# A one-core attention and expert kernel: spreads moved to the head of each slot, norm rows joined, transpositions in 64-row halves

## Chip, core and metric

One Trainium2 chip, one of its cores. The time is microseconds on the device for one execution, from the first to the last instruction and what lies around them; the median of several executions counts.

## What is computed

Input x is (4, 64, 128, 128) in float32: 4 images, 64 channels, 16384 pixels each.

```python
x = x + _L0_conv_ref(_ln_c(x), ...)     # linear attention, 8 heads, over the pixels of an image
t = _to_tokens(x)
t = t + _L0_ffn_ref(_ln_t(t), ...)      # top 2 of 8 experts per pixel, each 64 x 64
```

`_ln_c` and `_ln_t` normalise each pixel over its 64 channels. Attention: keys and queries are relu(W x + b), context = keys x values summed over an image's pixels, attended = context x queries, then a 1x1 convolution. Experts: softmax over the router's logits, the best two renormalised, sum of gate times (token @ expert_w + expert_b).

## The kernel before

The pixels of an image are cut in two halves (S = 2, on partitions 0-63 and 64-127), these in pieces of 1024 pixels (NP), so there are 32 **groups** of 2 x 1024 pixels. A hand-written software pipeline runs over 49 **steps** n of four **slots** k each. In step n each part works on its own group: `L_COLS`, `L_TURN` and so on say how many steps after its loading a group comes to it; the experts come last (`L_EXPERTS` = 17). Steps 17 to 31 hold all parts, the first 17 only the front, the last 17 chiefly routing and experts. A slot holds two **iterations** of the experts; an iteration is one pair of experts (of 4) for one u (512 of the 1024 pixels) of both halves.

Parts, with the lines of the profile:
- rows: square x on GpSimd (L422), TensorE sums it to rows of statistics (L986, copied by ScalarE L497), transposes them to columns (L1006, copied L504); VectorE makes the deviations (`x_deviations`, L654-657, and after ScalarE's root L642-644).
- `turn_x` (L911) transposes x, eight 128x128 blocks; VectorE multiplies by the deviation (`normalise`, L676) into xnT; `turn_back` (L921) transposes this back, ScalarE copies it to xn (L492).
- `make_keys` (L936, L943), `sum_up` (L974, keys times xnT; `add_sums` L688), `make_queries` (L960), `attend` (L1020), `residual` on VectorE (L720), its square on ScalarE (L532); `fold`, once per image, makes the attention matrix.
- routing: the same rows and columns for logits (L986, L515, L1006, L523); `gates`, 27 small VectorE operations for two groups at once, spread over slots by `gates_by_phase`, with ScalarE's root, exponent (L543) and two copies; `turn_gates` (L1045) makes rows of gates again, copied to `grows` (L565).
- experts: `broadcast` (L1059) spreads the gates of a pair over the partitions (the **spread**); for half s=0 VectorE multiplies (`product`, L816), for s=1 ScalarE copies (L571) and GpSimd multiplies (L431); `experts` multiplies the **products** by the weights (L1073, L1076) onto a bias (L1070); after four iterations `result` (L826) adds x1 and stores.

Each engine works in program order. PSUM has six rotating banks for all of this: `bank_uses` lists the uses in order, use i takes bank i mod 6, and TensorE may fill it when use i-6 has been read. The bias matmul waits for `result` of the former u. Rings of four tiles (`R_Z`) hold the products.

Within a slot each engine first did the slot's part, then the spread or product of the next slot's iterations, then TensorE the experts:

```python
                    for i in iterations(n, k + 1):
                        broadcast(i)
                    for i in iterations(n, k):
                        experts(i)
```

## Time and profile before

| | |
|---|---|
| median of 3 executions | 705.34 us (703.17 to 705.60) |
| profiled execution | 708.03 us, span 706.2 us |
| TensorE busy | 647.4 us (92%), mean granted clock 0.99 |
| VectorE | 532.2 us (75%) |
| ScalarE | 428.5 us (61%) |
| GpSimd | 396.5 us (56%) |
| DMA engines | about half busy |

The busy share of TensorE is that of matmuls that lie over one another, so it does not say how close the engine is to its peak; start-to-start distances are used below. "Idle" in a row is the time in which the row's engine stood still just before it, and the arrow names what ended that.

### The profile page before, as it was taken

What the parts mean: (1) busy time and instruction counts of PE and PEld (TensorE: products, weight loads), DVE (VectorE), ACT (ScalarE), POOL (GpSimd) and SP (SyncE); (2) the same over time, 40 slices, a digit from 0 to 9 for tenths busy, and PEclk for the clock granted to TensorE, in tenths of its full rate; (3) what the DMA queues carried; (4) which work ended last, traced back from release to release, by engine and by line L of the source; (5) the groups of instructions that cost most, each with busy time, mean ns of one, the idle gap of its engine ahead of it and who ended that gap; (6) DMA issues with size and microseconds to landing.
All of it is one profiled execution on the core that took longest, in us unless ns stands there. A gap on an engine that the chain in (4) does not pass through costs nothing.

```text
span 706.2 us, 20616 instructions
## 1 busy us (share of the span) xinstructions
PE 647.4 (92%) x7846; PEld 302.0 (43%) x7846; DVE 532.2 (75%) x1176; ACT 428.5 (61%) x852; POOL 396.5 (56%) x350
## 2 busy tenths in 40 slices
PE   3898999799999999999999999999989889896786
PEld 1676766444544444444544444444322223231221
DVE  3443456878788988888788988867889998978853
ACT  2354556857566676657576776756656666564542
POOL 7132342165456566565456566555657667575785
PEclk9999999999999999999999999999999999999999
DMA  6232544655565555555566564444656555454442
GB/s 141 61 75 71 130 122 122 169 145 123 136 151 135 136 140 125 127 136 123 133 150 148 123 148 99 98 111 107 149 130 152 120 120 135 102 131 97 107 104 46
DMA packets 32660, 86.16 MB, mean 122 GB/s; under 512 B 7650, under 2 KB 7826, under 8 KB 32562
## 3 DMA queue, kind: packets, MB, share of 16 engines
q1 hardware_dynamic: 32082, 84.64, 50.7%
q8 instruction: 63, 1.03, 0.7%
q0 software_dynamic: 288, 0.19, 0.1%
q14 instruction: 35, 0.29, 0.1%
q10 hardware_dynamic: 192, 0.01, 0.0%
HBM read 34.47 MB, written 16.78 MB: 73 GB/s over the span
## 4 chain that ended last, share of the span: by engine, by line
PE 68%; DVE 13%; ACT 10%; issue 7%; DMA 1%; POOL 1%; DVEq 0%; SPq 0%; ACTq 0%; POOLq 0%
PE bank L1073 25%; PE bank L1059 8%; PE bank L986 5%; PE bank L921 5%; PE bank L974 5%; PE bank L943 4%; PE bank L911 4%; ACT grows L565 3%; DVE z L816 3%; PE bank L1020 3%; PE bank L1006 2%; ACT L543 2%; DVE osb L826 2%; PE bank L1070 2%; DVE x L720 2%
## 5 line engine op out<-in xcount | busy, mean ns | idle before, releaser
L431 POOL TENSOR_TENSOR z<-gbs,x1d 128x512 f32<-128x512 f32 x256 | 320.6, 1275 | 220.7 <-ACT gbs L571 164.8
L1076 PE MATMUL bank<-z,ew 128*64 128x512 f32 x512 | 248.0, 607 | 0.0
L1073 PE MATMUL bank<-z,ew 128*64 128x512 f32 x512 | 247.9, 607 | 0.0
L571 ACT COPY gbs<-bank 128x512 f32<-128x512 f32 x256 | 140.0, 593 | 95.3 <-PE bank L1059 94.4
L816 DVE TENSOR_TENSOR z<-bank,x1d 128x512 f32<-128x512 f32 x256 | 162.9, 677 | 20.4 <-PE bank L1059 20.1
L1059 PE MATMUL bank<-grows,sel 64*64 64x512 f16 x1024 | 89.3, 388 | 28.2 <-DVE z L816 17.0
L422 POOL TENSOR_TENSOR xsq<-xin 128x512 f32<-128x512 f32 x64 | 65.6, 1046 | 81.8 <-DMA xin<-in_x_dram 78.2
L1073 PEld LDWEIGHTS bank<-z,ew 128*64 128x64 f32 x512 | 65.7, 138 | 105.6 <-issue 95.8
L492 ACT COPY xn<-bank 128x512 f32<-128x512 f32 x64 | 34.6, 588 | 68.2 <-PE bank L921 68.2
L676 DVE TENSOR_TENSOR xnT<-bank,rstd 128x512 f32<-128x512 f32 x64 | 41.3, 684 | 39.2 <-PE bank L911 37.0
L1059 PEld LDWEIGHTS bank<-grows,sel 64*64 64x64 f16 x1024 | 24.1, 104 | 97.2 <-issue 34.4
L1076 PEld LDWEIGHTS bank<-z,ew 128*64 128x64 f32 x512 | 65.6, 138 | 0.0
L826 DVE TENSOR_TENSOR osb<-bank,x 128x512 f32<-128x512 f32 x64 | 43.8, 685 | 23.1 <-PE bank L1076 23.1
L565 ACT COPY grows<-bank 128x1024 f16<-128x1024 f16 x32 | 32.3, 1010 | 30.3 <-PE bank L1045 30.3
L474 ACT ACTIVATE keys<-bank 128x512 f32<-128x512 f32 x64 | 34.8, 595 | 25.4 <-PE bank L943 25.4
L720 DVE SCALAR_TENSOR_TENSOR x<-bank,br_col,x_again 128x512 f32<-128x512 f32 x64 | 44.9, 743 | 5.2 <-PE bank L1020 4.8
L482 ACT ACTIVATE q<-bank,bq_col 128x512 f32<-128x512 f32 x64 | 40.6, 689 | 7.2 <-PE bank L960 7.2
L974 PEld LDWEIGHTS bank<-xnT,keys 128*64 128x64 f32 x1024 | 34.7, 139 | 13.3 <-issue 12.2
L974 PE MATMUL bank<-xnT,keys 128*64 128x66 f32 x1024 | 36.7, 225 | 1.2 <-ACT keys L474 1.0
L921 PE MATMUL bank<-k,xnT 128*128 128x128 f32 x256 | 35.9, 284 | 1.7 <-DVE xnT L676 1.2
L532 ACT ACTIVATE x1sq<-x 128x512 f32<-128x512 f32 x64 | 37.4, 645 | 0.0
L943 PEld LDWEIGHTS bank<-wk_bd,xn 64*64 64x64 f32 x2048 | 35.5, 135 | 4.2 <-issue 1.9
(138 smaller groups left out, 885.0 us busy)
## 6 DMA issues: line engine op xcount, KB each, us to landing
x1d<-x SPq DMA_DIRECT2D x128, 256.0 KB, 4.5
xin<-in_x_dram SPq DMA_DIRECT2D x64, 256.0 KB, 4.1
x_again<-in_x_dram SPq DMA_DIRECT2D x64, 256.0 KB, 4.1
out_dram<-osb SPq DMA_DIRECT2D x128, 128.0 KB, 2.4
k<-in_const_dram SPq DMA_DIRECT2D x1, 453.5 KB, 3.7
ew_nat<-in_L_ffn_expert_w_dram POOLq DMA_DIRECT2D x2, 64.0 KB, 6.5
sel<-in_const_sel_dram SPq DMA_DIRECT2D x1, 128.0 KB, 3.5
bk_rows<-bk_wide ACTq DMA_DIRECT2D x6, 1.0 KB, 1.7
```

Source lines behind the costliest of these rows:

```text
L422: pool.tensor_tensor(xsq[:, u * NT:(u + 1) * NT], half, half, ALU.mult).then_inc(x_squared, 1)
L431: pool.tensor_tensor(z[:, 1, i % R_Z, :], gbs[:, i % R_Z, :], x1d[:, g % 2, 1, u * NT:(u + 1) * NT], ALU.mult).then_inc(z_pool, 1)
L571: nc.scalar.copy(gbs[:, i % R_Z, :], bank[:, :]).then_inc(taken_of(("spread", i, 1)), 1)
L720: dve.scalar_tensor_tensor(x1[:, g % R_X1, half], bank[:, :], br_col[:, 0:1], x_again[:, g % 2, half], ALU.add, ALU.add).then_inc(taken_of ...
L816: dve.tensor_tensor(z[:, 0, i % R_Z, :], bank[:, :], x1d[:, g % 2, 0, u * NT:(u + 1) * NT], ALU.mult).then_inc(taken_of(("spread", i, 0)), 1)
L826: dve.tensor_tensor(osb[:, g % 2, half], out_bank[:, :], x1[:, g % R_X1, half], ALU.add).then_inc(out_done, 1)
L921: ins = pe.transpose(bank[:, j * P:(j + 1) * P], xnT[:, g % 2, u, j, 1:P + 1], eye)
L943: ins = pe.matmul(banks[s][C * a:C * a + C, j * C:(j + 1) * C], xn[rows, g % 2, j * P + C * a:j * P + C * a + C], wk_bd[rows, rows], start ...
L974: ins = pe.matmul(bank[C * s:C * s + C, 0:C + 2], keys[:, s, at:at + C], xnT[:, g % 2, u, j, C * s:C * s + C + 2], start=(u == 0 and j == ...
L1059: ins = pe.matmul(bank[cols, :], sel[rows, j, cols], grows[rows, g % 2, u * NT:(u + 1) * NT], start=True, stop=True)
L1073: pe.matmul(out_bank[0:C, :], ew[:, j, :], z[:, 0, i % R_Z, :], start=False, stop=(j == PAIRS - 1), skip_group_check=True).then_inc(prod_d ...
L1076: pe.matmul(out_bank[C:P, :], ew[:, j, :], z[:, 1, i % R_Z, :], start=False, stop=(j == PAIRS - 1), skip_group_check=True).then_inc(prod_d ...
```

## The change

- `L_TURN_GATES` goes from 16 to 17 and `L_EXPERTS` from 17 to 18: 50 steps.
- In every slot the spread (TensorE), the copy (ScalarE) and the product (VectorE) come first, before the slot's part; `product` on GpSimd already did.
- A spread of one iteration was two halves s by two column halves, eight 64x64 matmuls for two iterations. Now it is one matmul for each s, 32 rows deep and 128 columns wide; the second iteration takes its rows from `grows_again`, a copy of the gates on partitions 32-47 and 96-111, which two transfers on the Sync queue make for every group (`repeat_gates`). Two iterations use the array's four 32-row tiles.
- x's statistics and the router's rows go to one PSUM bank (`make_rows`), are copied, transposed and read together (`to_columns`, `take_cols`), in slot 1 instead of slot 0.
- `turn_x` and `turn_back` make 16 transpositions with 64 rows each, alternating between the row halves and two banks; `normalise` and the copy back take one half s or h each.
- Slot 1 of TensorE is now columns, gates' rows, turn back, sums; it was sums, turn back. Gates' rows move there from slot 3. The gate operations are dealt anew over the slots. `R_X1` is 8 (7).

```diff
 
-L_COLS, L_TURN, L_KEYS, L_AGAIN, L_ATTEND, L_ROUTE, L_GATES, L_TURN_GATES, L_EXPERTS = 1, 2, 3, 9, 11, 12, 14, 16, 17
+L_COLS, L_TURN, L_KEYS, L_AGAIN, L_ATTEND, L_ROUTE, L_GATES, L_TURN_GATES, L_EXPERTS = 1, 2, 3, 9, 11, 12, 14, 17, 18
 STEPS = GROUPS + L_EXPERTS
 ITERS = GROUPS * U * PAIRS
 
-R_X, R_Q, R_X1, R_Z = 3, 8, 7, 4
+R_X, R_Q, R_X1, R_Z = 3, 8, 8, 4
 
 
...
-            sel[hit & (kind == 0), p, m] = 1.0
-            sel[hit & (kind == 1), p, m] = LO
+            sel[hit & (kind % 4 == 0), p, m] = 1.0
+            sel[hit & (kind % 4 == 1), p, m] = LO
     return np.ascontiguousarray(f32), sel.reshape(P, PAIRS * P), np.eye(P, dtype=np.float16)
...
+            def repeat_gates(g):
+
+                when_taken(sp, ("gate_rows", g, 0))
+                if g == 0:
+                    sp.wait_ge(cleared, 4)
+                if g >= 2:
+                    for s in range(S):
+                        when_taken(sp, ("spread", (g - 1) * U * PAIRS - 1, s))
+                for s in range(S):
+                    sp.dma_start(grows_again[C * s + 32:C * s + 32 + 2 * E, g % 2, :],
+                                 grows[C * s:C * s + 2 * E, g % 2, :]).then_inc(grows_again_in[g % 2], 16)
...
         def quad_in(n, k, phase):
 
-            p, late = divmod(SLOTS * (n - L_GATES) + k - 1 - phase, 2 * SLOTS)
+            p, late = divmod(SLOTS * (n - L_GATES) + k - 3 - phase, 2 * SLOTS)
             return p if late == 0 and 0 <= p < GROUPS // 2 else None
 
...
+            def take_back(g, h):
+
+                bank = when_filled(act, ("back", g, h))
                 if g >= 2:
                     for s in range(S):
                         when_filled(act, ("queries", g - 2, s))
                         when_filled(act, ("keys", g - 2, s))
-                nc.scalar.copy(xn[:, g % 2, u * NT:(u + 1) * NT], bank[:, :]).then_inc(taken_of(("back", g, u)), 1)
-
...
+            def take_cols(n):
+
+                bank = when_filled(act, ("cols", n, 0))
+                columns = bank[:, 0:U * P].rearrange("p (a r) -> p a r", r=W)
+                g = n - L_ROUTE
+                if real(g):
+                    upto(act, gate_dve, (g // 2 - 2) * N_GATE + 8)
+                    half = g % 2 * U * NJ
+                    ins = nc.scalar.copy(lg[:, g // 2 % 2, half:half + U * NJ, :], columns[:, :, 0:NLG])
+                if real(n):
+                    upto(act, xstat_dve, n * N_XSTAT)
+                    ins = nc.scalar.copy(xs[:, :, :], columns[:, :, NLG:NROW])
+                ins.then_inc(taken_of(("cols", n, 0)), 1)
...
-            gate_steps = {0: root_dev, 5: exponent, 7: high, 8: low}
+            gate_steps = {0: root_dev, 4: exponent, 7: high, 8: low}
...
+            def normalise(g, s):
+
+                bank = when_filled(dve, ("turned", g, s))
                 dve.wait_ge(xstat_dve, (g + 1) * N_XSTAT)
                 if g >= 2:
                     when_filled(dve, ("sums", g - 2, 0))
-                dve.tensor_tensor(xnT[:, g % 2, u, :, 1:P + 1].rearrange("p j (s c) -> p j s c", s=S),
-                                  bank[:, :].rearrange("p (j s c) -> p j s c", j=NJ, s=S),
-                                  halves(rstd[:, g % 2, u, :]).unsqueeze(3).to_broadcast([P, NJ, S, C]), ALU.mult
-                                  ).then_inc(taken_of(("turned", g, u)), 1)
+                dve.tensor_tensor(xnT[:, g % 2, :, :, 1 + C * s:1 + C * s + C].rearrange("p u j c -> p (u j) c"),
+                                  bank[:, :].rearrange("p (a c) -> p a c", c=C),
+                                  rstd[:, g % 2].rearrange("p u (j s) -> p (u j) s", s=S)[:, :, s].unsqueeze(2)
+                                  .to_broadcast([P, U * NJ, C]), ALU.mult
+                                  ).then_inc(taken_of(("turned", g, s)), 1)
...
-            gates_by_phase = {8: (26, 27), 0: (0, 4), 2: (4, 9), 3: (9, 12), 4: (12, 16), 6: (16, 20), 7: (20, 26)}
+            gates_by_phase = {8: (26, 27), 0: (0, 4), 1: (4, 8), 2: (8, 13), 4: (13, 16), 5: (16, 18), 6: (18, 24), 7: (24, 26)}
...
                 if n == L_TURN:
                     set_weights()
                 for k in range(SLOTS):
+                    for i in iterations(n, k + 1):
+                        product(i)
+
                     if folding(n, k):
                         fold(*folding(n, k))
                     if k == 0 and real(n - L_EXPERTS - 1):
                         result(n - L_EXPERTS - 1, 1)
-                    if k == 1:
-                        if real(n - L_KEYS):
-                            add_sums(n - L_KEYS)
-                        if real(n - L_COLS):
-                            x_deviations(n - L_COLS, 0, 4)
+                    if k == 1 and real(n - L_KEYS):
+                        add_sums(n - L_KEYS)
                     if k == 2:
                         if real(n - L_EXPERTS):
                             result(n - L_EXPERTS, 0)
                         if real(n - L_ATTEND):
                             for u in range(U):
                                 residual(n - L_ATTEND, u)
-                    if k == 3 and real(n - L_COLS):
-                        x_deviations(n - L_COLS, 4, N_XSTAT)
                     for phase, (k0, k1) in gates_by_phase.items():
                         if quad_in(n, k, phase) is not None:
                             gates(quad_in(n, k, phase), k0, k1)
                     if k == 0 and real(n - L_TURN):
-                        for u in range(U):
-                            normalise(n - L_TURN, u)
-
-                    for i in iterations(n, k + 1):
-                        product(i)
+                        for s in range(S):
+                            normalise(n - L_TURN, s)
+                    if k == 1 and real(n - L_COLS):
+                        x_deviations(n - L_COLS, 0, 4)
+                    if k == 3 and real(n - L_COLS):
+                        x_deviations(n - L_COLS, 4, N_XSTAT)
             result(GROUPS - 1, 1)
 
...
+            def turn_x(g):
+
+                uses = [("turned", g, s) for s in range(S)]
+                banks = [when_free(pe, use) for use in uses]
+                for a in range(U * NJ):
+                    for s in range(S):
+                        rows = slice(C * s, C * s + C)
+                        ins = pe.transpose(banks[s][:, a * C:(a + 1) * C], xin[rows, g % R_X, a * P:(a + 1) * P],
+                                           eye[rows, rows])
+                        if a == U * NJ - 1:
+                            ins.then_inc(filled_of(uses[s]), 1)
+
+            def turn_back(g):
+
+                uses = [("back", g, h) for h in range(2)]
+                banks = [when_free(pe, use) for use in uses]
+                for s in range(S):
+                    when_taken(pe, ("turned", g, s))
+                for a in range(U * NJ):
+                    for h in range(2):
+                        rows = slice(C * h, C * h + C)
+                        ins = pe.transpose(banks[h][:, a * C:(a + 1) * C],
+                                           xnT[rows, g % 2, a // NJ, a % NJ, 1:P + 1], eye[rows, rows])
+                        if a == U * NJ - 1:
+                            ins.then_inc(filled_of(uses[h]), 1)
...
+            def make_rows(n):
+
+                use = ("rows", n, 0)
...
+                for part, (tile, weights) in enumerate(parts):
+                    chunks = tile.rearrange("p (u j n) -> p u j n", u=U, j=NJ)
                     for j in range(NJ):
-                        ins = pe.matmul(outs[j], weights, chunks[:, :, j, :], start=start, stop=not start,
-                                        skip_group_check=True)
+                        out_rows = bank[W * j:W * (j + 1), 0:U * P].rearrange("p (u n) -> p u n", u=U)
+                        ins = pe.matmul(out_rows, weights, chunks[:, :, j, :], start=(part == 0),
+                                        stop=(part == len(parts) - 1), skip_group_check=True)
                 ins.then_inc(filled_of(use), 1)
...
-                    use, rows = ("spread", i, s), slice(C * s, C * s + C)
+                if u == 0 and j == 1:
+                    pe.wait_ge(grows_again_in[g % 2], 32 * (g // 2 + 1))
+                source = grows_again if j % 2 else grows
+                for s in range(S):
+                    use = ("spread", i, s)
                     bank = when_free(pe, use)
-                    for a in range(2):
-                        cols = slice(C * a, C * a + C)
-                        ins = pe.matmul(bank[cols, :], sel[rows, j, cols], grows[rows, g % 2, u * NT:(u + 1) * NT],
-                                        start=True, stop=True)
-                    ins.then_inc(filled_of(use), 1)
+                    first = C * s + 32 * (j % 2)
+                    pe.matmul(bank[:, :], sel[first:first + 32, j, :],
+                              source[first:first + 32, g % 2, u * NT:(u + 1) * NT], start=True, stop=True
+                              ).then_inc(filled_of(use), 1)
 
...
                 if n == L_EXPERTS - 1:
                     pe.wait_ge(set_pool, N_SET_POOL)
                 for k in range(SLOTS):
+                    for i in iterations(n, k + 1):
+                        broadcast(i)
+
                     if folding(n, k):
                         fold(*folding(n, k))
                     if k == 0:
                         if real(n - L_KEYS):
                             make_keys(n - L_KEYS)
-                        if real(n - L_COLS):
-                            g = n - L_COLS
-                            to_columns(("stat_cols", g, 0), stat_rows, ("stat_rows", g, 0))
-                        if real(n - L_ROUTE - L_COLS):
-                            g = n - L_ROUTE - L_COLS
-                            to_columns(("route_cols", g, 0), route_rows, ("route_rows", g, 0))
                         if real(n - L_TURN):
-                            for u in range(U):
-                                turn_x(n - L_TURN, u)
+                            turn_x(n - L_TURN)
                     if k == 1:
+                        if has_rows(n - L_COLS):
+                            to_columns(n - L_COLS)
+                        if real(n - L_TURN_GATES):
+                            turn_gates(n - L_TURN_GATES)
+                        if real(n - L_TURN):
+                            turn_back(n - L_TURN)
                         if real(n - L_KEYS):
                             sum_up(n - L_KEYS)
-                        if real(n - L_TURN):
-                            for u in range(U):
-                                turn_back(n - L_TURN, u)
                     if k == 2:
                         if real(n - L_ATTEND):
                             attend(n - L_ATTEND)
                         if real(n - L_KEYS):
                             make_queries(n - L_KEYS)
-                    if k == 3:
-                        if real(n - L_TURN_GATES):
-                            turn_gates(n - L_TURN_GATES)
-                        if real(n):
-                            measure_x(n)
-                        if real(n - L_ROUTE):
-                            route(n - L_ROUTE)
-
-                    for i in iterations(n, k + 1):
-                        broadcast(i)
+                    if k == 3 and has_rows(n):
+                        make_rows(n)
+
                     for i in iterations(n, k):
                         experts(i)
```

TensorE in the first part of the program, one step of the front before: keys (`wk_bd`), columns (`stat_rows`), turn (`xin`), sums (`keys`), back (`xnT`), queries, rows.

```order
L936 MATMUL bank<-bk_rows,ones 64x512 x4
L943 MATMUL bank<-wk_bd,xn 64x64 x32
L1006 MATMUL bank<-k,stat_rows 128x128 x2
L911 MATMUL bank<-k,xin 128x128 x8
L974 MATMUL bank<-xnT,keys 64x66 x16
L921 MATMUL bank<-k,xnT 128x128 x8
L960 MATMUL bank<-xn,wq 64x512 x4
L986 MATMUL bank<-xin,k 32x256 x4
L986 MATMUL bank<-xsq,k 32x256 x4
```

The same step after, where L919 is turn, L1020 the columns, L933 back and L988 the sums.

```order
L950 MATMUL bank<-bk_rows,ones 64x512 x4
L957 MATMUL bank<-wk_bd,xn 64x64 x32
L919 MATMUL bank<-k,xin 128x64 x16
L1020 MATMUL bank<-k,rows_sb 128x128 x2
L933 MATMUL bank<-k,xnT 128x64 x16
L988 MATMUL bank<-xnT,keys 64x66 x16
L974 MATMUL bank<-xn,wq 64x512 x4
L1010 MATMUL bank<-xin,k 32x256 x4
L1010 MATMUL bank<-xsq,k 32x256 x4
```

The columns stand behind the turn, and the sums, which stood between turn and back, behind both.

VectorE in a step with all parts, from slot 1's products to slot 2's result, before.

```order
L816 TENSOR_TENSOR z<-bank,x1d 128x512 x2
L688 TENSOR_TENSOR s_acc<-bank,s_acc 128x66
L654 SCALAR_TENSOR_TENSOR xstat<-xs 128x16
L655 TENSOR_TENSOR xstat<-xstat,xs 128x16
L656 TENSOR_SCALAR xstat<-xstat 128x16
L657 RECIPROCAL xstat<-xstat 128x16
L762 TENSOR_REDUCE gstat<-bank 128x32
L765 TENSOR_TENSOR gk<-bank,gstat 128x256
L788 SCALAR_TENSOR_TENSOR bank<-gk,bank 128x256
L762 TENSOR_REDUCE gstat<-bank 128x32
L816 TENSOR_TENSOR z<-bank,x1d 128x512 x2
L826 TENSOR_TENSOR osb<-bank,x 128x512
```

The same place after, from slot 1's sums, which its two products (L823) precede, to slot 2's result, where L823 is the product, L833 the result and L769 to L775 are gate operations.

```order
L695 TENSOR_TENSOR s_acc<-bank,s_acc 128x66
L790 TENSOR_TENSOR bank<-bank,rb_row 128x256
L769 TENSOR_REDUCE gstat<-bank 128x32
L775 TENSOR_TENSOR bank<-bank,gstat 128x256
L766 SCALAR_TENSOR_TENSOR bank<-bank,k 128x256
L769 TENSOR_REDUCE gstat<-bank 128x32
L660 SCALAR_TENSOR_TENSOR xstat<-xs 128x16
L661 TENSOR_TENSOR xstat<-xstat,xs 128x16
L662 TENSOR_SCALAR xstat<-xstat 128x16
L663 RECIPROCAL xstat<-xstat 128x16
L823 TENSOR_TENSOR z<-bank,x1d 128x512 x2
L833 TENSOR_TENSOR osb<-bank,x 128x512
```

The products stand first in each slot; `s_acc` comes behind slot 1's, and five gate operations and four deviations stand between it and slot 2's.

VectorE late in the program, the slots around the last gate operations of the last pair, before: products (L816), result (L826), gates (L745, L799, L749).

```order
L745 TENSOR_TENSOR bank<-bank,gstat 128x256
L799 TENSOR_TENSOR bank<-bank,bstat 128x256
L816 TENSOR_TENSOR z<-bank,x1d 128x512 x2
L749 TENSOR_TENSOR bank<-bank,gT 128x512
L816 TENSOR_TENSOR z<-bank,x1d 128x512 x2
L826 TENSOR_TENSOR osb<-bank,x 128x512
L816 TENSOR_TENSOR z<-bank,x1d 128x512 x4
L826 TENSOR_TENSOR osb<-bank,x 128x512
```

And after: products (L823), result (L833), gates (L752, L806, L756).

```order
L823 TENSOR_TENSOR z<-bank,x1d 128x512 x2
L833 TENSOR_TENSOR osb<-bank,x 128x512
L752 TENSOR_TENSOR bank<-bank,gstat 128x256
L806 TENSOR_TENSOR bank<-bank,bstat 128x256
L823 TENSOR_TENSOR z<-bank,x1d 128x512 x2
L756 TENSOR_TENSOR bank<-bank,gT 128x512
L823 TENSOR_TENSOR z<-bank,x1d 128x512 x2
L833 TENSOR_TENSOR osb<-bank,x 128x512
```

Before, a result stood ahead of its own slot's two products (`x4` are two of its slot and two of the next); after, it stands behind them, while on TensorE the bias waits for it in the same slot as before.

## Rows read from the trace of the kernel before

**Rows 1.** Busy time by stretch: stretch, length, per engine busy us (count), clock, DMA.
```profile
0.00:145.20 145.20, 124.45 (x2298) 84.16 (x2299) 73.38 (x234) 77.92 (x175) 49.11 (x66) 0.99 0.48 115
145.20:460.80 315.60, 311.20 (x3903) 148.65 (x3902) 264.29 (x577) 211.04 (x424) 189.95 (x158) 1.00 0.56 131
460.80:706.20 245.40, 211.69 (x1651) 69.19 (x1649) 194.53 (x366) 139.55 (x255) 157.44 (x126) 0.98 0.49 114
```

**Rows 2.** Timeline, TensorE: start, us, line, operation, count; steps 17 and 33.
```profile
145.17 1.04 PE L911 MATMUL bank<-k,xin 128*128 128x128 f32 x8
...
460.77 1.04 PE L911 MATMUL bank<-k,xin 128*128 128x128 f32 x8
```

**Rows 3.** Timeline of one middle step, TensorE and one row of VectorE.
```profile
401.39 1.10 PE L943 MATMUL bank<-wk_bd,xn 64*64 64x64 f32 x64
402.42 0.44 PE L1006 MATMUL bank<-k,stat_rows 128*128 128x128 f32 x2
...
402.91 1.04 PE L911 MATMUL bank<-k,xin 128*128 128x128 f32 x8
403.88 0.63 PE L1059 MATMUL bank<-grows,sel 64*64 64x512 f16 x8
...
406.39 1.10 PE L974 MATMUL bank<-xnT,keys 128*64 128x66 f32 x32
...
407.42 1.09 PE L921 MATMUL bank<-k,xnT 128*128 128x128 f32 x8
407.54 0.23 DVE L688 TENSOR_TENSOR s_acc<-bank,s_acc 128x66 f32<-128x66 f32 x1 [0.83 <-PE bank L974]
...
408.45 0.63 PE L1059 MATMUL bank<-grows,sel 64*64 64x512 f16 x8
...
415.85 0.62 PE L1045 MATMUL bank<-eye,gT 128*128 128x128 f16 x8
416.40 0.64 PE L986 MATMUL bank<-xin,k 128*32 128x256 f32 x8
...
418.26 0.63 PE L1059 MATMUL bank<-grows,sel 64*64 64x512 f16 x8
```

**Rows 4.** Timeline of one front step: turn, normalise, back.
```profile
65.84 1.04 PE L911 MATMUL bank<-k,xin 128*128 128x128 f32 x8
66.48 1.29 DVE L676 TENSOR_TENSOR xnT<-bank,rstd 128x512 f32<-128x512 f32 x2 [2.72 <-PE bank L911]
...
68.00 1.09 PE L921 MATMUL bank<-k,xnT 128*128 128x128 f32 x8
```

**Rows 5.** Timeline of the last two steps, slot 3 and slot 0.
```profile
689.53 0.63 PE L1059 MATMUL bank<-grows,sel 64*64 64x512 f16 x8 [1.10 <-ACT grows L565]
...
690.03 1.29 DVE L816 TENSOR_TENSOR z<-bank,x1d 128x512 f32<-128x512 f32 x2 [3.14 <-PE bank L1059]
690.08 0.64 PE L1073 MATMUL bank<-z,ew 128*64 128x512 f32 x1
...
691.42 0.59 PE L1073 MATMUL bank<-z,ew 128*64 128x512 f32 x1
...
691.95 0.63 PE L1059 MATMUL bank<-grows,sel 64*64 64x512 f16 x8
692.09 0.69 DVE L826 TENSOR_TENSOR osb<-bank,x 128x512 f32<-128x512 f32 x1 [0.78 <-PE bank L1076]
...
692.84 0.41 PE L1070 MATMUL bank<-grows,eb_rows 128*64 128x512 f16 x2 [0.26 <-DVE osb L826]
693.08 0.59 PE L1073 MATMUL bank<-z,ew 128*64 128x512 f32 x1
```

**Rows 6.** Timeline of VectorE, a gate operation at 548.53.
```profile
548.53 1.17 DVE L734 SCALAR_TENSOR_TENSOR bstat<-lg 128x32 f32<-128x32 f32 x1
```

**Rows 7.** Groups by line: out<-in, shapes, count, busy us, mean ns, idle before.
```profile
L768 DVE TENSOR_TENSOR bank<-bank,gstat 128x256 f32<-128x256 f32 x32 | 13.8, 432 | 11.6 <-ACT gex L543 11.0
...
L543 ACT ACT_TABLE_LOAD x16 | 20.5, 1283 | 0.3
```

154 lines of the change are left out of this document (60 added, 94 removed).

## The prediction

> **What bounds it now.** I read the busy time in three stretches first [rows 1]. In the middle one, where all parts of the pipeline run, TensorE is busy 311.2 of 315.6 us at a clock of 1.00, VectorE 264.3. The transposition blocks of x, one for each of the 32 groups and one a step, mark the steps: that of step 17 starts at 145.2, that of step 33, the last, at 460.8 [rows 2], so 16 steps of 19.7 us. Before 145.2 only the front of the pipeline runs; after 460.8 mostly experts (TensorE 211.7 of 245.4, VectorE 194.5). VectorE has 264.3 / 16 = 16.5 us of work a step against 19.7: only three us of idle time, and it takes its work strictly in program order. So the second view is the timeline: which VectorE result stands between two blocks of TensorE.
>
> **What TensorE saves.** (a) Spreading. A slot's spread is now two quads of 64x64 tiles: 0.55 us from its start to the next block (689.53 to 690.08) [rows 5]. The change issues one quad of four 32-row tiles with 128 output columns. No row has this form. Bounds: 0.33 (half of 0.55, and 0.05 for the change of tiling), or, without overlap, four times the 0.24 of one quad (0.55 less 0.07, halved), 0.96. I take 0.33, since the four 64x64 tiles of make_keys do run together (64 records in 1.03 us) [rows 3]: 4 x 0.22 = 0.9 us a step. The Trainium skill ("TensorE: Matmul & The Clock Gate", measured speedup of packing) gives 3.07 times for four row tiles of 512 columns; by it a spread would be about 0.31. No run here shows it yet.
> (b) Norm rows. One pair of 128x128 transpositions instead of two pairs: 0.27 saved once routing runs (402.42 to 402.91 is 0.49 for four) [rows 3]. The row matmuls stay.
> (c) Transpositions in halves. Eight of x now take 0.97, eight back 1.03 (402.91 to 403.88, 407.42 to 408.45) [rows 3]. Then there are 16, each loading 128 columns and streaming 64 instead of 128, in pairs of row halves. Bounds: about 0.55, if streaming limits now and halves; 0.97, if loading limits and the two of a pair overlap; 1.9, if they do not. The keys' 64 records of four tiles start 0.016 us apart on average, against 0.12 for one transposition over the whole array [rows 3], so loads and streams of different tiles overlap there, which speaks against 1.9. Between the other two nothing decides; I take the middle, 0.74, two blocks a step. At 0.97 the sum would grow by 10 us (0.46 in 15 front steps, 0.23 in 15 middle ones), at 0.55 shrink by 8.
> The Trainium skill ("TensorE: Matmul & The Clock Gate", LDWEIGHTS) says that a load takes its time by its columns, whatever the rows, and further down that loads overlap when their row groups differ: by the first rule alone this block would take 1.9 (rival 3), by both 0.97.
> Together 0.9 + 0.27 + 0.5 = 1.7 us a step, so at most 18.0 of TensorE's own work, and 17.5 with the present waits taken out. If nothing waited, that would be the new period.
>
> **What it moves, and what is then late.** Let t be the start of the spread of slot 0, "last" the start of a slot's last expert matmul.
> Slot 0. VectorE takes its first product 0.50 after the spread starts, two products take 1.2 (689.53 and 690.03; 1.29 wide, the next operation starts 0.1 earlier) [rows 5], and only then result(u=1); from that to the bias matmul are 0.75, to the experts 0.24 (692.09, 692.84, 693.08) [rows 5]. So the experts start at t + 0.5 + 1.2 + 0.75 + 0.24 = t + 2.7. TensorE's keys and transposition hide this (0.33 + 1.27 + 0.74). From the first to the last expert matmul 1.3 (690.08, 691.42) [rows 5], from there to the next spread 0.53 (691.95): slot 0 takes 4.5.
> Slot 1. Products run from 5.0 to 6.2. TensorE does columns 0.27, gate transpositions 0.55 (415.85) [rows 3], back 0.74, and only then the sums: start 6.4. add_sums starts 1.15 after that (406.39 and 407.54) [rows 3], at 7.5. It stands right behind the products in VectorE's queue, so VectorE idles 1.3 us; before, the sums were first. Behind it wait five gate operations, 0.46 each from start to start (width 0.43 in [rows 7]), 2.3 to 2.8, and four deviations, 0.8. VectorE is free at about 11.0. TensorE spreads slot 2 at 9.25.
> Slot 2. The first product comes at 11.0 instead of 9.75. The first bank of the queries is that product's: TensorE waits. Products, result, bias: 11.0 + 1.2 + 0.75 = 12.95, experts 13.2, next spread at 15.0. The slot takes 5.75, 1.25 more than with a punctual product.
> Slot 3. 0.33 + 1.8 for the row matmuls (416.40 to 418.26) [rows 3] + 1.8 of experts: the step ends at 19.0.
> Two additions. In every other step VectorE carries the rest of a gate pair and its first four operations in slot 3; one of these, of 32 columns, took 1.17 beside a GpSimd product [rows 6], where 256 columns take 0.43 [rows 7], and the next may too. It enters the next step about 0.8 late, and what hangs on result in slot 0 moves with it. And the exponent's table load of 1.28 [rows 7] with its two activations, together some 1.9 us of ScalarE, now precedes the next slot's copies, which the first transposition bank waits for: 0.7 in every second step. So 19.0 + (0.8 + 0.7) / 2 = 19.8; with folds 19.9. The saved 1.7 us are eaten by the waits.
>
> **Front.** Now transposition of x to transposition back takes 2.16 us (65.84, 68.00) [rows 4], and the sums (1.1) lie under the 1.3 us of normalise. After, both normalises start when the whole block is done, only the columns (0.27) lie under them, and the sums come behind. Start to start becomes about 2.3 (0.95 until the block is done, 1.3 and a start), +0.14, and the sums' 1.05 come on top; against that stand the cheaper back block (-0.29) and the columns' 0.27, now covered. 0.14 + 1.05 - 0.29 - 0.27 is +0.6 a step for nine steps, and +0.5 for six with routing (its columns saved as well); the clearing of grows_again on GpSimd ahead of its loads +1: 9.4. And one step more runs without experts (8.6 + 0.5): 9.1. Step 18's block of x, the first beside experts, starts at 145.2 + 18.5 = 163.7.
> **Middle.** 15 steps of 19.9 instead of 16 of 19.7: 298.5 - 315.6 = -17.1.
> **End.** The waits of slots 0 and 2 have no cover here. Now a slot without a result takes 2.4 (689.53 to 691.95), and one with it about 0.5 more, since its bias starts 0.9 behind the spread (692.84) [rows 5]. After, from the last expert start of slot 1: 0.53, 0.50, 1.2, 0.75, 0.24 and 1.28 to the next last one = 4.5, against 2.15 for the others: 13.3 to 13.9 a step at the very end (about 10.7 to 12.5 now). With gates and attention a step is 4.5, then 0.33 + 0.27 + 0.55 + 1.8 = 3.0, then 4.5 and 1.1 because gate work makes slot 2's product late (9.0 or 8.5 for 7.95), then 0.33 + 0.9 + 1.8 = 3.0: 16.1, and up to 16.5 with the contention, against a present mean of 245.4 / 16 = 15.3. From step 33's turn on: 17.5 for its rest (a middle step without x's rows and the part before the turn), 16.7 for step 34 (keys, no turns), 8 x 16.45, four steps of about 15.4 in which attention and then gates run out (61.5), 2 x 13.85, and 17 for the last with its store: 272 against 245.4, +26.6.
>
> The grows_again transfers are costed at nothing: gates are copied in slot 1, 7 us before slot 3 needs them; if late they would cost a store's landing, 2.4 us a step. Larger rings cost nothing.
> **Sum.** 18.5 - 17.1 + 26.6 = +28.0. The profiled execution is 708.03 (span 706.2), 2.7 above the median of 705.34; +28.0 on the median gives 733.
>
> **Rivals.**
> 1. *TensorE stays the bound, faster.* Everything hangs on VectorE reaching slot 2 late. If gates and deviations fit under the experts (no wait for sums, no contention), a step takes 17.5: 15 x 2.4 = 36 us less, 697. For it: VectorE has 16.5 us of work, below 17.5. Against it: add_sums standing in front. It decides at a step of 18.0; below that the kernel is faster. Chance 0.14.
> 2. *Gain and loss cancel.* Streaming limits the halves (0.55: 8 less) and VectorE is late by less, a middle step of 18.6 (20 less): 705. Chance 0.08.
> 3. *The packing does not pack.* Four 32-row tiles one after another: +0.63 a slot, 128 slots, most of it on the path, +60: about 793. Or halves that do not overlap: 32 blocks twice at +1.15, about +50: 780. Together 0.10; the overlapping of the keys' tiles speaks against both.
> 4. *The forecast*: slower, 733, its own range 714 to 756. Chance 0.68.
>
> **Numbers.** Range 702 to 758: it leaves out rival 3 and most of rival 1. Faster by over 0.5% (about what a measurement of this kernel can tell): 0.16; within: 0.06; slower: 0.78.
>
> **What the profile would show.** Middle steps of 19.9 us (right) or under 18 (rival 1); TensorE idle before the queries' matmuls released by the VectorE product, and before the bias by osb; about 1.3 us a step before s_acc, released by the sums (0.8 now). Spread to next block 0.33, halves' block 0.74. At the end, spreads alternately 4.5 and 2.15 apart. I am wrong if VectorE idles less than half a us before s_acc, or if the last 17 steps take less than 255 us.

## The result, and the profile after

The changed kernel takes 794.4 us (median of four executions), the kernel before 705.5 beside it: ratio 1.126, 95% interval 1.120 to 1.131, 89 us slower. I had forecast +28. The profiled execution has a span of 791.6 against 706.2.

The first view is the three stretches again, cut at x's transposition block of step 18 and of step 33 (columns as in [rows 1]):

```profile
0.00:169.60 169.60, 129.55 (x2713) 82.51 (x2715) 81.64 (x254) 84.53 (x186) 52.96 (x70) 0.95 0.43 105
169.60:506.30 336.70, 280.56 (x3635) 121.54 (x3633) 271.16 (x543) 195.62 (x386) 178.23 (x149) 0.95 0.51 119
506.30:791.60 285.30, 215.71 (x1471) 68.75 (x1466) 204.90 (x381) 141.94 (x263) 167.07 (x134) 0.93 0.46 107
```

Cut at the same two blocks, the kernel before has 164.9, 295.9 and 245.4. TensorE has less work (625.8 us busy in all, 647.4 before) and yet a longer middle: 280.6 us busy of 336.7. And its granted clock, 1.00 in the middle of before [rows 1], is now 0.95. The forecast had 163.7, 298.5 and 272, so it missed 6, 38 and 13 us. The view of the waits says where TensorE stands still (engine and line, what for, us in total, times, longest):

```profile
PE bank L1086 <- DVE osb L833: 63.4, 31, 3.1
...
DVE s_acc L695 <- PE bank L988: 47.4, 28, 3.3
...
PE bank L974 <- DVE z L823: 31.6, 13, 3.3
```

These are the three waits of the forecast: bias for `result`, `add_sums` for the sums, queries for slot 2's product. What they cost shows in the timeline of an even step (n even: the rest of a gate pair is made), from the spread of slot 1 to that of slot 3:

```profile
443.82 0.39 PE L1075 MATMUL bank<-grows,sel 32*128 32x512 f16 x2
...
446.84 0.23 DVE L695 TENSOR_TENSOR s_acc<-bank,s_acc 128x66 f32<-128x66 f32 x1 [1.30 <-PE bank L988]
...
447.41 2.04 POOL L437 TENSOR_TENSOR xsq<-xin 128x512 f32<-128x512 f32 x2
447.43 0.43 DVE L772 TENSOR_TENSOR bank<-bank,gstat 128x256 f32<-128x256 f32 x1
...
448.44 0.39 PE L1075 MATMUL bank<-grows,sel 32*128 32x512 f16 x2
...
448.83 0.66 DVE L803 TENSOR_SCALAR gstat<-gstat 128x32 f32<-128x32 f32 x1
...
449.56 2.48 POOL L446 TENSOR_TENSOR z<-gbs,x1d 128x512 f32<-128x512 f32 x2
449.80 1.06 DVE L660 SCALAR_TENSOR_TENSOR xstat<-xs 128x16 f32<-128x16 f32 x1
450.89 1.19 DVE L661 TENSOR_TENSOR xstat<-xstat,xs 128x16 f32<-128x16 f32 x1
452.11 0.17 DVE L662 TENSOR_SCALAR xstat<-xstat 128x16 f32<-128x16 f32 x1
...
452.49 1.22 DVE L823 TENSOR_TENSOR z<-bank,x1d 128x512 f32<-128x512 f32 x2
...
453.17 1.09 PE L974 MATMUL bank<-xn,wq 64*64 64x512 f32 x8 [3.32 <-DVE z L823]
...
454.79 1.06 PE L1089 MATMUL bank<-z,ew 128*64 128x512 f32 x1
...
458.02 0.39 PE L1075 MATMUL bank<-grows,sel 32*128 32x512 f16 x2
```

Slot 2 takes 9.58 us (448.44 to 458.02), forecast 5.75. Two things are to be seen. Two deviations of 16 columns (L660, L661), 0.11 to 0.18 us each where GpSimd is idle, take 1.06 and 1.19 while GpSimd multiplies. And the expert matmuls behind the wait take 1.06 instead of 0.59. The next view is the granted clock (the third number from the right), stretch by stretch of the same step; its last row is a slot 0 near the end, 591.6 to 597.7:

```profile
448.40:453.10 4.70, 1.45 (x14) 0.31 (x12) 4.53 (x9) 2.57 (x4) 3.54 (x4) 1.00 0.03 7
453.10:458.00 4.90, 4.73 (x18) 1.14 (x18) 3.29 (x7) 2.34 (x4) 0.00 (x0) 0.65 0.44 101
458.00:462.00 4.00, 4.00 (x46) 1.52 (x44) 3.41 (x6) 2.48 (x5) 2.52 (x2) 1.00 1.05 241
...
591.63:597.74 6.11, 4.14 (x16) 0.97 (x15) 2.66 (x5) 2.50 (x5) 2.97 (x3) 0.72 0.84 201
```

Behind 3.3 us in which TensorE stood idle, it runs partly at 1.2 GHz instead of 2.4: the mean is 0.65 of full speed over 4.9 us. Below, "half clock" is this.

### The profile page after: what moved, and what is told of

The parts are those of the page before. It is cut to its first block, busy times and chain, and to the rows that moved or that the text cites. A ratio compares the mean times of both kernels' runs of the same rounds, so it can differ in the third digit from the quotient of the medians.

```text
span 791.6 us, 20634 instructions
## 1 busy us (share of the span) xinstructions
PE 625.8 (79%) x7806; PEld 272.8 (34%) x7806; DVE 557.7 (70%) x1176; ACT 422.1 (53%) x832; POOL 398.3 (50%) x351
## 4 chain that ended last, share of the span: by engine, by line
PE 48%; DVE 33%; issue 12%; ACT 3%; DVEq 1%; ACTq 0%
PE bank L1089 19%; DVE z L823 7%; PE bank L1010 5%; PE bank L988 5%; DVE osb L833 4%; PE bank L1075 3%; PE bank L933 3%; PE bank L1086 3%; PE bank L974 3%; DVE xnT L682 2%; DVE bstat L784 2%; DVE gstat L769 2%; PE bank L919 2%; PE bank L1059 1%; DVE xstat L662 1%
## 5 line engine op out<-in xcount | busy, mean ns | idle before, releaser
L1092 PE MATMUL bank<-z,ew 128*64 128x512 f32 x512 | 264.9, 643 | 0.0
L1089 PE MATMUL bank<-z,ew 128*64 128x512 f32 x512 | 264.9, 643 | 0.0
L823 DVE TENSOR_TENSOR z<-bank,x1d 128x512 f32<-128x512 f32 x256 | 162.7, 677 | 100.5 <-PE bank L1075 100.4
L1089 PEld LDWEIGHTS bank<-z,ew 128*64 128x64 f32 x512 | 69.3, 145 | 103.1 <-issue 85.0
L1086 PE MATMUL bank<-grows,eb_rows 128*64 128x512 f16 x128 | 28.0, 434 | 64.6 <-DVE osb L833 63.4
L1092 PEld LDWEIGHTS bank<-z,ew 128*64 128x64 f32 x512 | 69.3, 145 | 0.0
L974 PE MATMUL bank<-xn,wq 64*64 64x512 f32 x256 | 39.0, 681 | 31.7 <-DVE z L823 31.6
L1075 PE MATMUL bank<-grows_again,sel 32*128 32x512 f16 x256 | 51.4, 395 | 1.0 <-DVE x L727 1.0
L1075 PE MATMUL bank<-grows,sel 32*128 32x512 f16 x256 | 51.0, 395 | 0.0
L1075 PEld LDWEIGHTS bank<-grows,sel 32*128 32x128 f16 x256 | 12.1, 91 | 112.8 <-issue 105.5
L833 DVE TENSOR_TENSOR osb<-bank,x 128x512 f32<-128x512 f32 x64 | 43.5, 679 | 5.6 <-PE bank L1092 5.6
L1034 PE MATMUL bank<-q,att 64*64 64x512 f32 x256 | 39.3, 688 | 9.3 <-issue 9.3
L1086 PEld LDWEIGHTS bank<-grows,eb_rows 128*64 128x64 bf16 x128 | 7.2, 109 | 96.8 <-DVE osb L833 92.7
L933 PE MATMUL bank<-k,xnT 64*128 64x64 f32 x512 | 24.2, 236 | 20.1 <-DVE xnT L682 20.1
```

What stands on the lines that cost most here:

```text
L823: dve.tensor_tensor(z[:, 0, i % R_Z, :], bank[:, :], x1d[:, g % 2, 0, u * NT:(u + 1) * NT], ALU.mult).then_inc(taken_of(("spread", i, 0)), 1)
L833: dve.tensor_tensor(osb[:, g % 2, half], out_bank[:, :], x1[:, g % R_X1, half], ALU.add).then_inc(out_done, 1)
L933: ins = pe.transpose(banks[h][:, a * C:(a + 1) * C], xnT[rows, g % 2, a // NJ, a % NJ, 1:P + 1], eye[rows, rows])
L974: ins = pe.matmul(banks[s][cols, :], wq_4[rows, cols], xn[rows, g % 2, u * NT:(u + 1) * NT], start=True, stop=True)
L1075: pe.matmul(bank[:, :], sel[first:first + 32, j, :], source[first:first + 32, g % 2, u * NT:(u + 1) * NT], start=True, stop=True).then_inc ...
L1086: pe.matmul(out_bank[cols, :], eb_rows[:, cols], grows[:, g % 2, u * NT:(u + 1) * NT], start=True, stop=False, skip_group_check=True)
```

## The experiments

Times are medians beside the kernel before on the same chip (704 to 708 us). The three stretches of each profiled execution, cut as above:

| kernel | ratio to before (95%) | median | to step 18 | to step 33 | rest |
|---|---|---|---|---|---|
| before | 1 | 704-708 | 164.9 | 295.9 | 245.4 |
| changed | 1.126 (1.120-1.131) | 794.4 | 169.4 | 336.7 | 285.5 |
| spreading last | 1.126 (1.124-1.129) | 797.2 | 166.0 | 390.6 | 240.5 |
| attention repeated | 1.125 (1.121-1.129) | 794.5 | 167.7 | 335.6 | 288.8 |
| short squares | 1.101 (1.099-1.103) | 778.8 | 168.6 | 324.2 | 284.2 |
| deviations late | 1.073 (1.069-1.076) | 757.6 | 172.3 | 300.5 | 282.6 |
| sums first | 1.067 (1.060-1.073) | 749.2 | 158.6 | 305.1 | 283.3 |
| sums first, deviations late | 1.046 (1.044-1.049) | 736.8 | 158.8 | 292.0 | 284.5 |
| sums first, spreading last | 1.003 (1.000-1.005) | 704.9 | 156.8 | 307.2 | 235.4 |
| sums first, deviations and gates late | 1.085 (1.080-1.090) | 762.4 | 163.2 | 308.4 | 288.5 |

### Spreading last again

On TensorE, and likewise for the copies, the products and in `bank_uses`:

```diff
-                    for i in iterations(n, k + 1):
-                        broadcast(i)
-
                     if folding(n, k):
...
                         make_rows(n)
 
+                    for i in iterations(n, k + 1):
+                        broadcast(i)
```

> Undoes one part alone: the spreading of the gates, its copies on ScalarE and its products on VectorE stand at the end of a slot again, as before the change; the four 32-row tiles, the joined norm rows, the transpositions in halves and the moved gate phases stay. Theory (the order of the spreading makes the waits, the new forms save): the blocks measured in the changed kernel are 0.23 (spread, four a step), 0.27 (columns) and 0.72 (two blocks in halves) cheaper than before, 1.9 us a step, so a middle step of about 17.8 instead of 19.7 while VectorE's 16.5 to 17 us allow it, and the whole 650 to 680 us. Rival (the new forms themselves cost the time, the order is harmless): about 794 us.

797.2 us. That is the rival's number, but not for the rival's reason: two opposite effects happen to cancel. The rest fell by 45 us, below before, and the middle rose by 54. The timeline of one of its middle steps:

```profile
435.32 0.23 DVE L695 TENSOR_TENSOR s_acc<-bank,s_acc 128x66 f32<-128x66 f32 x1 [2.78 <-PE bank L987]
...
437.94 0.92 DVE L660 SCALAR_TENSOR_TENSOR xstat<-xs 128x16 f32<-128x16 f32 x1
...
439.89 0.96 DVE L662 TENSOR_SCALAR xstat<-xstat 128x16 f32<-128x16 f32 x1
...
441.74 1.14 PE L973 MATMUL bank<-xn,wq 64*64 64x512 f32 x8 [3.25 <-DVE z L823]
```

The sums had stayed behind columns, gate transpositions and the transposition back, and VectorE now stands 2.8 us for them. So "the order" was at least two edits, not one: the place of the spreading and the place of the sums.

### TensorE kept busy through the wait

```diff
+WARM = (4, 2)
...
+                times = 1 if g + L_ATTEND < L_EXPERTS else WARM[(g + L_ATTEND) % 2]
+                for again in range(times):
+                    for u in range(U):
```

> Adds work and leaves all else alone: from the first step with experts on, the eight attention matmuls of a step are issued four times in even steps and twice in odd ones, into the same banks, ahead of the queries, where TensorE waits 3.3 and 1.9 us for VectorE. The output is the same. Theory (the long wait lets the clock fall, and the half clock costs slot 2 of an even step about 1.4 us beside the wait): the granted clock in the experts behind the wait is 1.00 instead of about 0.65, the even middle steps fall from 23.1 to about 21.8, and the whole is 10 to 20 us less, 775 to 785. Rival (the clock costs nothing that the wait does not hide): 794 or more.

794.5, no change in all: the rival's number. In the steady even steps the mechanism is there: slot 2 fell from 9.58 to 7.99 us (446.71 to 454.70), with the clock at 1.00 behind a wait that is now 0.75:

```profile
446.71 0.39 PE L1079 MATMUL bank<-grows,sel 32*128 32x512 f16 x2
...
451.45 1.09 PE L975 MATMUL bank<-xn,wq 64*64 64x512 f32 x8 [0.75 <-DVE z L824]
...
454.70 0.39 PE L1079 MATMUL bank<-grows,sel 32*128 32x512 f16 x2
```

Slot 0 of the next step grew from 4.84 to 5.40, which leaves 1.0 for a pair of steps. In slot 2 of the steps with a fold it lost up to 3.8 us (14.05 for 10.22, spread to spread), and the rest got 3 longer, which eats it. So the half clock costs slot 2 of a steady even step 1.6 us; that the kernel as a whole could win anything this way isn't shown, since the repeated matmuls are work of their own.

### GpSimd's squares cut short

```diff
-                half = xin[:, g % R_X, u * NT:(u + 1) * NT]
+                part = slice(u * NT, u * NT + (NT if g == 0 else 32))
+                half = xin[:, g % R_X, part]
```

> Leaves work out: GpSimd squares only the first 32 of each 512 columns of x (all of them for the first group), so the norm statistics are wrong; all else is as in the changed kernel. Theory (VectorE's small operations with both operands in SBUF stand still beside GpSimd's squares and products): the two deviations of 1.06 and 1.19 us in slot 1 of an even step fall to 0.2 to 0.4 where the squares were what they met, slot 2 of an even step falls from 9.5 to 7 or 7.5, the even step to about 21, and the whole to 765 to 780. Rival (they meet the products as well, or it is their own chain that takes the time): 790 to 795.

778.8: within the theory's range. The spreads of the even step at 425.6 are 4.86, 4.63, 6.55 and 4.06 apart (20.1 in all, 23.1 before the edit). GpSimd's product stands where it stood, 1.12 us behind the spread (436.24; 449.56 before the edit). But L803 takes 0.18 instead of 0.66, so that two deviations are done ahead of it; the third still meets it:

```profile
436.36 1.18 DVE L663 TENSOR_SCALAR xstat<-xstat 128x16 f32<-128x16 f32 x1
```

The four deviations take 1.74 instead of 2.69. In another even step all of this is the same to 0.01 us, the wait before the queries too (1.88 and 1.89), but its slot 2 takes 8.16 (392.18 to 400.34). The views of these two slots differ in the granted clock, 0.79 and 1.00:

```profile
392.18:400.34 8.16, 6.17 (x32) 1.45 (x30) 6.35 (x14) 4.91 (x8) 2.49 (x2) 0.79 0.27 66
435.12:441.67 6.55, 4.56 (x32) 1.11 (x31) 6.34 (x14) 3.84 (x6) 2.50 (x2) 1.00 0.15 34
```

So the half clock alone costs such a slot 1.61 us, and it comes behind a wait of 1.9 us in one step and not in the next. Some odd steps have it now too and grew from 21.2 to 22.8.

### Deviations behind slot 2's product, sums first, and both

The first on VectorE (ScalarE's root goes behind its queries as well), the second on TensorE and in `bank_uses`:

```diff
-                    if k == 1 and real(n - L_COLS):
+                    if k == 2 and real(n - L_COLS):
                         x_deviations(n - L_COLS, 0, 4)
...
                     if k == 1:
+                        if real(n - L_KEYS):
+                            sum_up(n - L_KEYS)
                         if has_rows(n - L_COLS):
```

> A reordering alone: the first four deviations of x move from the end of slot 1 to the end of slot 2 on VectorE, behind slot 2's product, and ScalarE takes their root behind the queries. Output the same. Theory (what stands ahead of slot 2's product is what TensorE waits for): 1.2 to 2.3 us leave the way to the queries, slot 2 falls to about 7 in even and 5.5 in odd steps, with the clock at 1.00; middle steps of about 20.7 and 20.2, the whole 755 to 775. Rival (the gates or the sums are what is late, or the deviations are as late in slot 3): 785 to 795.

> Undoes one part alone: TensorE makes the sums of slot 1 first again, ahead of the columns, the gate transpositions and the transposition back (the banks in that order too); VectorE's order is as in the changed kernel, with the spreading first. Theory (add_sums stands idle 1.3 us behind the sums and pushes gates, deviations and slot 2's product): the idle time before s_acc (47 us in all) falls below 15, slot 2 falls by 1.3 or more in both kinds of step, the even one's by up to 2.7 if the clock stays full; middle steps of about 21 and 20, the whole 755 to 775. Rival (the wait for the sums only moves to another one, of VectorE for the columns or of TensorE for a bank): 785 to 795.

> The two reorderings together: sums first in TensorE's slot 1, and x's first four deviations at the end of slot 2. Theory (both are waits of one chain, which then is left with the gates alone): less than each alone, 735 to 750, middle steps of 19 or under. Rival (they overlap: once the deviations are away, the sums' wait is free): as with the deviations alone, 755 to 760.

757.6, 749.2 and 736.8: 37, 45 and 58 us less, the second more than its theory's range gave, the other two within theirs. Together they give less than the sum of 82, as waits of one chain do. Sums first takes 10.8 us from the front, 31.6 from the middle and 2 from the rest; VectorE's idle time before s_acc falls from 47 to 6.6 us and TensorE's before the queries from 31.6 to 9.4. In a front step the block of x now follows after 6.72 us (70.61 to 77.33) instead of 7.19 (66.82 to 74.01). With both edits the middle takes less than before's 295.9, by the windows of that kernel with the clock nearly full:

```profile
158.80:450.80 292.00, 267.85 (x3630) 121.40 (x3631) 259.36 (x543) 195.27 (x385) 178.55 (x149) 0.99 0.58 137
```

### Spreading last with the sums first

> Puts the spreading, its copies and its products at the end of a slot, as in the run with the spreading last, and the sums first in slot 1. With the spreading last alone the middle steps took 25 to 27 us and the last ones 11 to 15; its timeline shows VectorE idle 2.8 us before s_acc and three deviations of 0.92 to 0.96 each behind it. Theory (not the place of the spreading but what stands ahead of it in slot 1 makes the product of slot 2 late): the middle steps fall by more than 4 us, to 20 to 22, the whole to 690 to 730. Rival (the late place of the spreading itself is what the middle cannot bear): 770 or more.

704.9, the time of before and within the theory's range. The edit is the first experiment's, on top of the sums first; against the sums first alone it is worth 44 us, 48 of them in the rest and -2 in the middle (by its profiled execution, which took 701.4, 3.5 less than the median). The windows of its middle and rest:

```profile
156.80:464.10 307.30, 282.58 (x3634) 129.00 (x3632) 240.89 (x542) 194.20 (x385) 179.21 (x148) 1.00 0.55 130
464.10:699.50 235.40, 212.77 (x1475) 71.78 (x1475) 190.71 (x384) 143.69 (x265) 167.60 (x134) 0.99 0.55 129
```

Near the end the bias waits little for `result`, since product and copy were made a slot's experts earlier; in the changed kernel (second fence) it waits 1.97:

```profile
628.45 0.41 PE L1085 MATMUL bank<-grows,eb_rows 128*64 128x512 f16 x2 [0.49 <-DVE osb L833]
```

```profile
743.84 0.39 PE L1075 MATMUL bank<-grows,sel 32*128 32x512 f16 x2
746.20 0.41 PE L1086 MATMUL bank<-grows,eb_rows 128*64 128x512 f16 x2 [1.97 <-DVE osb L833]
748.25 0.39 PE L1075 MATMUL bank<-grows,sel 32*128 32x512 f16 x2
```

### Gates late

```diff
-            gates_by_phase = {8: (26, 27), 0: (0, 4), 1: (4, 8), 2: (8, 13), 4: (13, 16), 5: (16, 18), 6: (18, 24), 7: (24, 26)}
+            gates_by_phase = {8: (26, 27), 0: (0, 4), 1: (4, 8), 2: (8, 10), 3: (10, 13), 4: (13, 16), 5: (16, 18), 6: (18, 20), 7: (20, 26)}
```

> As the two reorderings together, and besides most gate operations of slot 1 move to slot 2, behind its product: phases 2 and 6 keep two operations each (8 to 10, 18 to 20), phases 3 and 7 take the rest. Theory (whatever VectorE does ahead of slot 2's product is paid by TensorE): slot 2 takes 4.6 in both kinds of step, the middle step about 18.5, the whole 15 to 25 us below the run without this. Rival (the work comes back as lateness in slot 3 or slot 0, since VectorE is now the fuller engine): within 5 us of that run, or above it.

762.4, 26 us more than without it. Slot 2 is 4.42 in both kinds of step, as the theory had it, but the even step's next slot 0 takes 9.0 to 9.4 instead of, mostly, 6.3: the rival. What is taken from ahead of one product arrives ahead of another.

### Four more on the kernel with sums first and spreading last

The first of them is this. The second, on top of it, moves one call on ScalarE, and the third, on top of the second, one on VectorE. The fourth stands alone and puts the two quads of 64x64 back:

```diff
+            gates_by_phase = {8: (26, 27), 0: (0, 4), 2: (4, 9), 3: (9, 12), 4: (12, 16), 6: (16, 20), 7: (20, 26)}
...
+            gate_steps = {0: root_dev, 5: exponent, 7: high, 8: low}
```

> On top of the run with the spreading last and the sums first (704.9 us), the gate operations stand in the slots of a step as before the change (phases 2, 3, 4, 6, 7 with 5, 3, 4, 4 and 6 operations; the exponent on ScalarE at phase 5). There an even step has four gate operations ahead of slot 2's product instead of six, and the exponent's table load of 1.28 us, which that run's timeline shows ahead of the copies of the keys, stands behind them. Theory (what is ahead of slot 2's product and of the copies that TensorE waits for is paid): 0.5 to 1 us a step less over some 25 steps, 680 to 697. Rival (that run is bound by something else, such as VectorE's sum of work): 700 to 708.

> As the kernel with the old gate phases, and besides ScalarE takes the root of x's deviations behind the queries instead of ahead of them, so that its table load of 1.28 us doesn't stand between the queries' matmuls and their copies. Theory (the row matmuls wait 0.7 us for those copies in even steps): 3 to 10 us less than the kernel with the old gate phases. Rival (the row matmuls then wait for something else, and VectorE's root comes late in slot 3): within 3 us of it.

> As the kernel with the late root, and besides VectorE makes x's first four deviations behind slot 2's product (which stands at the end of slot 1) instead of ahead of it. Theory (they stand on the way to the queries' bank, alone 0.8 and beside GpSimd's work up to 3 us): 3 to 15 us less than the kernel with the late root. Rival (behind the product they delay the result and with it the bias of slot 2's experts by as much as they free the queries): the same within 3 us.

All three theories missed: 721.9, 727.0 and 729.0 us (ratios 1.025, 1.031 and 1.035, intervals 0.003 to each side). The first two fit their rivals no better; the third, 2.0 us above the second, is its rival's. The table of the first isn't quite that of before either: it has the old phases, but they count from slot 3, where a pair's gates begin since the change, and not from slot 1. The old gate phases left the middle at 306.2 and made the rest 257.0 instead of 235.4; the two edits behind them lengthen the middle by 4 each.

The trace of the first shows where the 21.6 us of the rest are. TensorE waits for the bank that VectorE's product holds, without the edit (first line) and with it:

```profile
PE bank L1074 <- DVE z L823: 2.4, 12, 0.2
```

```profile
PE bank L1074 <- DVE z L823: 13.0, 11, 2.2
```

Ahead of such a product stand small gate operations beside GpSimd:

```profile
560.04 1.29 DVE L784 TENSOR_TENSOR bstat<-bstat,lg 128x32 f32<-128x32 f32 x1
```

It takes 0.19 alone, and the next one, at 561.37, 1.18 instead of 0.18. And 27 expert matmuls of the rest start 0.85 apart instead of 0.43, against 4 without the edit: some 10 us, an estimate from the count. So it's the two costs of the changed kernel again, at another place; no run takes them out one by one there.

> On top of the run with the spreading last and the sums first (704.9 us), the spread goes back to two quads of 64x64 tiles instead of one quad of four 32-row tiles; the repeated rows are still sent, but not read. Theory (the new form saves 0.23 us a spread, and in most slots TensorE is what the others wait for): 0.23 x 128 = 29 us at the most, so 715 to 733. Rival (VectorE bounds the middle, and the saving is hidden): up to 712.

709.3 (1.007, interval 1.004 to 1.009): 4.4 us more, hardly clear of the noise (1.000 to 1.005 without it). The 0.23 us of a spread are hidden in most slots; the rival.

### The new forms in the order of before

The order slot by slot: keys, columns, transposition; sums, transposition back; gate transpositions, attention, queries; rows; and the spread last in each. Besides:

```diff
-L_COLS, L_TURN, L_KEYS, L_AGAIN, L_ATTEND, L_ROUTE, L_GATES, L_TURN_GATES, L_EXPERTS = 1, 2, 3, 9, 11, 12, 14, 17, 18
+L_COLS, L_TURN, L_KEYS, L_AGAIN, L_ATTEND, L_ROUTE, L_GATES, L_TURN_GATES, L_EXPERTS = 1, 2, 3, 9, 11, 12, 14, 16, 17
```

> The new forms (four 32-row tiles, joined norm rows, transpositions in halves) in the order of before: spreading, copies and products last in a slot, sums first in slot 1, columns in slot 0, gate table and deviations at their old places, experts 17 steps behind again. Only the gate transpositions stand elsewhere, first in slot 2 instead of slot 3, so that the rows can be sent again in time. Theory (TensorE was the bound of before and the forms save it 1.9 us a step, of which VectorE's work and waits let about half through): middle steps of 18.2 to 19, the end 10 to 15 us shorter, the whole 670 to 692. Rival (the chain over VectorE binds at the same 19.7 as soon as TensorE is cheaper): 697 to 707.

> As the new forms in the order of before, but the spread is two quads of 64x64 tiles again (the repeated rows are still sent, and not read). Theory (with this order TensorE is the bound, so that a spread's 0.23 us are all paid): 15 to 29 us more than the kernel with the new forms in the order of before. Rival (as in the run with the same edit on the other order, which cost 4 us): at most 6 us more.

> As the new forms in the order of before, but TensorE makes the sums of slot 1 behind the transposition back. Theory (VectorE has its sums first in the slot and stands still for them, then is late with gates, deviations and the next product; in the front the sums lengthen the chain from step to step): 25 to 60 us more than the kernel with the new forms in the order of before. Rival (the sums cost only together with the columns in slot 1 or the moved gate table): under 15 us more.

> As the new forms in the order of before, but spreading, copies and products stand first in each slot. Theory (in the last steps TensorE has no other work to cover product, result and bias: 13.8 to 18 us a step with the spreading first, 11 to 14.5 with it last, in the runs so far): 30 to 50 us more than the kernel with the new forms in the order of before, nearly all of it behind step 33. Rival (the cost was that of the late slot 2 under the moved gate table): under 15 us more.

722.3 (1.026, interval 1.024 to 1.028), 727.6, 770.4 and 834.3 us. The first is slower than before, and slower than both its theory and its rival had it. It carries a wait that I had put there myself by moving the gate transpositions to slot 2: TensorE's for ScalarE's low gate parts, in its page's group of these transpositions:

```profile
L1056 PE MATMUL bank<-eye,gT 128*128 128x128 f16 x256 | 22.1, 236 | 42.9 <-ACT gT L566 42.9
```

Its steps are 18.6 us where that wait is absent and 22.3 where it stands (before: 19.5 to 19.7). On top of it the 64x64 spread costs 5.4 us (rival), the sums last 48 (theory: 21 in the front, 24 in the middle, 3 in the rest), and the spreading first 112, far above its theory: 62 in the rest, the expected part and more, and 43 in the middle. In that last kernel the waits for the gate parts (56.4) and, new, for the repeated rows (15.3) take part in it, so 112 is no clean price of the spreading.

> As the new forms in the order of before, but the gate transpositions are first in slot 3, as before the change, and the repeated rows are sent behind the other loads of the step; the first odd pair of a group reads the rows themselves, since the repeated ones are not there yet. Theory (the forms save TensorE 1.9 us a step and about 1.1 of it reaches the step where no new wait stands in the way, as the odd steps of 18.6 show): even and odd middle steps of 18.5 to 18.9, the whole 672 to 692, faster than before. Rival (another wait takes the place of the one for the gates, and the even steps stay above 20): 698 or more.

> As the run with the gate transpositions in slot 3, but the spread is two quads of 64x64 tiles (the repeated rows are still sent, and not read). Theory (TensorE is the bound, a spread's 0.23 us are paid in most of the 128 slots): 12 to 29 us more. Rival (VectorE's product follows the first of the two spreads anyway and hides the rest): at most 6 us more, as the two earlier pairs with this edit gave (4 and 5 us).

788.2 (1.119, interval 1.114 to 1.125) and 783.3 (1.113, interval 1.109 to 1.117): the first far into its rival, the second 5 us below the first. The reason stands in the first's groups:

```profile
L1073 PE MATMUL bank<-grows_again,sel 32*128 32x512 f16 x192 | 48.3, 428 | 90.3 <-DMA grows_again<-grows 83.7
```

Queued on SyncE behind the x1d copies, the repeated rows land too late for the fourth iteration of a group, the first that reads them, and TensorE waits 83.7 us for them in all. The second kernel keeps that wait (75.0 us), so it says nothing on the tiles. Whether the new forms gain in the order of before, with no wait added, stays open: it wasn't tried in a form free of one.

## Why the prediction was wrong

**What held.** TensorE's savings: a spread is followed by the next block 0.32 us later (448.44, 448.76; forecast 0.33), the halves' blocks take 0.64 (forecast 0.74), and the columns take 0.27 instead of 0.49, so 0.22 less; the forecast had 0.27 less. In a front step of the changed kernel the block of x, its columns, the block back and the sums start at:

```profile
66.82 0.71 PE L919 MATMUL bank<-k,xin 64*128 64x64 f32 x16
67.46 0.44 PE L1020 MATMUL bank<-k,rows_sb 128*128 128x128 f32 x2
...
69.00 0.71 PE L933 MATMUL bank<-k,xnT 64*128 64x64 f32 x16 [1.10 <-DVE xnT L682]
69.64 1.15 PE L988 MATMUL bank<-xnT,keys 128*64 128x66 f32 x32
```

So rival 3, whose 793 the time happens to meet, is refuted: everything packs, and the 64x64 spread put back costs 4.4 us more, not less. Rivals 1 and 2 fall with the stretches: the middle step is 22.4, and both needed one below 19. Neither of the forecast's two signs of being wrong showed. The mechanism of the forecast held too: sums last makes `add_sums` idle 1.30 us (forecast 1.3), gates and deviations follow, slot 2's product is late, then queries, `result`, bias and experts. Taking the sums' place back gave 45 us, the deviations' 37, the spreading's 44 with the sums first. At the very end spreads are 4.41 and 2.20 apart (743.84, 748.25; 741.64, 743.84), forecast 4.5 and 2.15.

**The step that failed** is the size of slot 2, and with it the middle step: "19.0 + (0.8 + 0.7) / 2 = 19.8; with folds 19.9". It measured 23.1 and 21.2 by turns, 22.4 with folds. In the even step the spread of slot 0 was at 438.95, so in my count VectorE was to be free at 11.0 and the next spread to come at 15.0; they came at 13.5 (452.49) and 19.1. Of the 4.1 us:
- The four deviations took 2.69 (449.80 to 452.49), forecast 0.8: +1.9. I had priced what VectorE's small operations lose beside GpSimd as half of 0.8 a step, in slot 3 alone, from the one row of 1.17 [rows 6]. The squares cut short and the deviations moved each took much of this away: slot 2 of even steps at 6.55, where the clock held, and at 5.3.
- The experts behind the wait took 3.2 (454.79 to 458.02), forecast 1.8: +1.4 for the half clock, which the forecast had at 1.00 throughout. The run with repeated attention gave 1.6 of slot 2 back. Over the whole middle 21 expert matmuls start about 0.85 apart instead of 0.43, so the half clock is some 8 of its 38 us, an estimate from the count.
- The rest, 0.8, is `add_sums` at 7.9 instead of 7.5, six gate operations for five, and the 0.66 of L803 beside the squares.

In odd steps slot 1 takes 5.77 (forecast 4.75), since the normalisation is late behind gate statistics of the same kind, and slot 2 6.54 (5.75).

The same operations in groups over the whole run (busy us, mean ns), of before:

```profile
L643 DVE TENSOR_TENSOR xstat<-xstat 128x16 f32<-128x16 f32 x32 | 19.9, 623 | 1.1
...
L654 DVE SCALAR_TENSOR_TENSOR xstat<-xs 128x16 f32<-128x16 f32 x32 | 7.0, 218 | 9.5 <-ACT xs L504 9.5
L655 DVE TENSOR_TENSOR xstat<-xstat,xs 128x16 f32<-128x16 f32 x32 | 5.6, 174 | 1.1
...
L643 DVE TENSOR_TENSOR bstat<-bstat 128x32 f32<-128x32 f32 x16 | 4.1, 254 | 0.6
```

And of the changed kernel:

```profile
L649 DVE TENSOR_TENSOR bstat<-bstat 128x32 f32<-128x32 f32 x16 | 17.3, 1081 | 0.6
...
L661 DVE TENSOR_TENSOR xstat<-xstat,xs 128x16 f32<-128x16 f32 x32 | 12.7, 396 | 1.1
L660 DVE SCALAR_TENSOR_TENSOR xstat<-xs 128x16 f32<-128x16 f32 x32 | 12.0, 376 | 10.7 <-ACT xs L527 10.7
...
L649 DVE TENSOR_TENSOR xstat<-xstat 128x16 f32<-128x16 f32 x32 | 6.4, 200 | 1.1
```

Nothing in them was changed but the moment at which they run. Before had this loss too, on the deviations of slot 3 (0.62), where less waits for them; it has moved to the first deviations and the gate statistics, ahead of products. So the price stood in the profile before, and the forecast took one row of it. The timeline shows what they wait for: L660 ends at 450.86 and L661 at 452.08, and GpSimd's two products, 1.24 each from 449.56, end at 450.80 and 452.04. One small operation waits out one GpSimd operation. It isn't luck of one step: of the operations on 16 or 32 columns, reciprocals aside, 97 begin beside a GpSimd multiplication in the changed kernel, and 89 of these take over 0.4 us; of the 194 that begin outside one, none does. (Before: 49 of 53, and none of 245.)

The Trainium skill ("SBUF — State Buffer", Who interferes with whom) says that a VectorE instruction with two SBUF inputs contends with a GpSimd one that reads SBUF, and that the later one is blocked until the first has ended. By that rule each of the two ends with one of GpSimd's products; the trace agrees, within 0.06 us. The same section of the Trainium skill would have VectorE's products undisturbed, one of whose inputs lies in PSUM: they keep 0.68 before and after.

**Front.** Step 18's block came at 169.4, forecast 163.7. The miss isn't where the forecast added its small terms. Up to step 15's block (125.1, before 121.3) the change cost 3.8 us, forecast 8.4: nine steps at 0.6, four at 0.5, and 1. The steps 15, 16 and 17 then took 11.7, 13.8 and 18.8, together 44.3, where the forecast had 34.0 (9.6, 15.3 and 9.1). The term that failed is the added step "without experts (8.6 + 0.5): 9.1": the gates, the first spreads and their products run in it. The clock falls there too. These are the windows of this step and of the last one ahead of the experts in the kernel before, 0.82 and 1.00:

```profile
150.60:169.40 18.80, 12.68 (x204) 7.63 (x200) 13.64 (x38) 12.03 (x27) 3.55 (x4) 0.82 0.74 175
```

```profile
130.30:145.20 14.90, 10.18 (x187) 6.51 (x186) 12.04 (x36) 11.95 (x25) 2.62 (x3) 1.00 0.86 202
```

Putting the sums first gave back 10.8 in the front, 5.4 of it in these three steps. What the half clock and the waits cost there each, no run separates.

**End.** It took 285.3, forecast 272, +13.3. A slot 0 of 6.1 us (591.63 to 597.74, clock 0.72) shows the step that failed: from its spread to its first expert matmul it takes 2.65, forecast 2.7, and from there to the next spread 3.46, forecast 1.8. The waits were priced right, the clock was not. In the whole end 36 expert matmuls start about 0.85 apart instead of 0.43, some 15 us (before: 11, some 4). That is as much as the miss; as a sum it is counted, not tested, for other waits moved as well.

**What became of TensorE's 1.9 us a step.** With the two orders undone the kernel has the time of before and not less, it seems because nearly every block that got shorter stood beside a VectorE result, not on it. For the spread that is shown: its whole packing, 29 us of TensorE's time by 0.23 x 128, is worth 4.4 and 5.4 us in two orders. The columns and the transpositions were never put back, so for them it is only argued. What costs the middle of that kernel its 11 us against before is open. By the stretches, spreading first up to step 33 with sums first and deviations late (158.8 and 292.0), and spreading last from there on (235.4), would come to 686, an estimate; it wasn't tried.

## What to carry to other kernels

Before TensorE work is made cheaper, ask what it waits for next: here the spread stood beside a VectorE chain, and the saving of 1.9 us a step was not seen in the time. In an engine that works in program order, price whatever comes ahead of the operation that others wait for, and ask what each of these meets on other engines at its new moment: an operation of 0.17 us can cost 1.2. Count such operations by the moment, not by their mean: the profile before had the price. A wait costs more than its length where the clock falls behind it. And undoing one edit of a pair can leave the time where it was, so read the stretches and undo the edits in both orders before naming one.

## What was unexpected of the hardware

- VectorE's operations on 16 or 32 columns with all inputs in SBUF take 0.11 to 0.19 us alone and up to 1.3 beside a running GpSimd multiplication, also with a single input (L662, 0.96 in the run with the spreading last). Reciprocals don't: 0.35 at 449.53, and so all nine of the changed kernel that begin beside GpSimd. Those of 256 columns ran undisturbed (0.43 at 447.43), with one operand in PSUM.
- After 3.3 us of TensorE idling the granted clock was 0.65 over the next 4.9 us, at 1.00 again 5 us later, and after 0.75 us it stayed at 1.00. After the same wait of 1.97 us it was 0.72 in the slot from 591.63 and 1.00 in the one from 743.84, and after 1.9 us 0.79 and 1.00 in the run with the squares cut short: the length of the last wait alone doesn't tell.
- Four 32-row tiles of 512 columns start to the next block in 0.32 us against 0.55 for two quads of 64x64; sixteen half-height fp32 transpositions of 64 columns take 0.64 against 0.97 for eight full ones.
